# Set-up of a Mamba and expert block: weights loaded, folded and used in another order

## The chip, the cores and the metric

One core of a Trainium2 chip runs the whole program in one launch. The metric is the device time of one execution in microseconds. The core has five engines with an instruction queue each: PE (TensorE), DVE (VectorE), ACT (ScalarE), POOL (GpSimd) and SP (SyncE, which here only issues DMA transfers). They wait for each other by semaphores.

## What is computed

64 samples, each of 16 image tokens and 32 text tokens of width D = 192, go through an embedding, a two-way Mamba mixer and a layer of eight experts (two for each token). Cut to what matters here:

```python
# image: patches of 768 values, layer norm with gamma, beta, then a projection
h_img = _layernorm(patch) * gamma @ W_proj.T + (beta @ W_proj.T + b_proj)
# text: a token's row, a segment's row and two time embeddings (sine of an angle, last column linear)
angle = tau * w_tau + b_tau
h_txt = tok_rows + alpha_age * sin(angle_age) + alpha_abs * sin(angle_abs) + alpha_seg * seg_rows
x1 = _layernorm(h)
# mixer: x1 @ bm_in -> halves for the two directions -> Mamba (in_w, conv, silu, B, C, dt, scan, gate, out_w) -> bm_out
u = silu(conv(x)); dt = softplus(...); state = exp(dt * A) * state + dt * u * B; y = sum(state * C)
h2 = ln_g * _layernorm(mixer + x1) + ln_b + h
out = h2 + experts(_layernorm(h2))
```

Two weights are products that the kernel makes once at the start. `wxz` is the outer input projection times the Mamba's own (`bm_in` by `inT`, eight groups: two directions, two halves of the output, two halves of the contraction). `w2t` is the Mamba's output projection times the outer one (`outw` by `bmoT`). The layer norm of the image is folded too: `gw` is gamma times the projection, `proj_sum` its column sums, `proj_bias` is beta times the projection plus the bias.

## The kernel before

The tokens are cut into eight chunks of 384 (8 samples by 48). A chunk goes through the front (embedding, x1, its transpose `xT`), then for each direction through `xz` (PE: xT by wxz), the convolution (PE, with diagonal matrices `tap_diag`), silu, `bc`, `dt`, and 12 units of scan. A unit is 4 of 16 states by 128 of 384 channels: POOL makes the input `ring` = dtu times B (L645), ACT the decay in the two PSUM tiles `states` (L629, L632), DVE scans (L656) and multiplies by C (L658), PE sums over the states (L668). B and C come as broadcasts from DRAM (`brep`, `crep`, spread by SP, L608).

The order of all engines is written out by hand. Each engine first runs its own set-up function, then `program`: a list of steps `early()`, a wait for the whole set-up (`set_up`), `prologue()` (front and first direction of chunk 0), and a plan for each chunk. An engine takes from the list those steps for which it has a function.

The set-up before: SP issues all loads from one list (L839), `bm_in` and `inT` first, with a semaphore of their own (`fold_in`); behind them ids, taus and the patches of chunk 0 (`ptok`, `pT`, L275 to L278); then all others, which share one semaphore, `w_in`. PE folds eight groups into eight PSUM banks (L883), ACT copies each to `wxz` (L907). DVE waits for all of `w_in` (L862), makes the diagonals, `gw` and `betas`, and then takes up the patches. PE then makes proj_sum, proj_bias, the image (L311) and, still ahead of the embedding, the output weights' product (L897), which ACT copies to `w2t` behind the sine. POOL first gathers the text rows (L286), then waits for `w_in` and makes the angles `theta` (L336).

Of the kernel before, what the change touches and what calls it, by code (L numbers as in the profile page):

```python
# [22 lines left out]
KH = D // 2  # L23
# [48 lines left out]
def build_mamba(nc, a, dram, ident, logits, sem):  # L72

    with ExitStack() as ctx:
# [101 lines left out]
        fold_in = sem("folded_weights_loaded")  # L176
        w_in = sem("weights_loaded")
# [634 lines left out]
        def dve_router(v, c):  # L812
# [5 lines left out]
        loads = [  # L818
            (bm_in.rearrange("p d j k -> p (d j k)"), a["bm_in"]), (inT.rearrange("p j o -> p (j o)"), a["inT"]), (outw.rearrange("p j o -> p (j o)"), a["outw"]),
            (bmoT.rearrange("p j o -> p (j o)"), a["bmoT"]), (projT.rearrange("p k o -> p (k o)"), a["projT"]),  # L820
            (tgam, a["tgam"]), (tbet, a["tbet"]), (projb, a["projb"]),
            (xpw[:, :, 0:2 * NS], a["xpw_bc"]), (xpw[:, :, 2 * NS:2 * NS + R], a["xpw_dt"]), (dtw[2 * NS:2 * NS + R, :], a["dtw"]), (dtb[:], a["dtb"]),
            (cw[:].rearrange("p o k -> p (o k)"), a["cw"]), (cb[:], a["cb"]), (dskip[:], a["dskip"]),
            (aneg[:].rearrange("p o n -> p (o n)"), a["a_log"]),
            (w_tau[:].rearrange("p s k -> p (s k)"), a["w_tau"].partition_broadcast(128)),
            (b_tau[:].rearrange("p s k -> p (s k)"), a["b_tau"].partition_broadcast(128)),
            (alpha[:], a["alpha"].partition_broadcast(128)),
            (outb[:], a["outb"]), (ln_g[:], a["ln_g"].partition_broadcast(128)), (ln_b[:], a["ln_b"].partition_broadcast(128)),
            (rw[:].rearrange("p k e -> p (k e)"), a["rw"]),
        ]  # L830
        FOLDED = 2
        LOADED = 16 * (len(loads) - FOLDED)
        banks = [py] + [s[:, 512 * i:512 * i + 512] for s in states for i in range(2)] + [pf[0], pf[1], pq]

        def sp_setup(sp):
            for i, (dst, src) in enumerate(loads):
                if len(dst.shape) == 2 and len(src.shape) == 3:
                    src = src.rearrange("p a k -> p (a k)")
                sp.dma_start(dst, src).then_inc(w_in if i >= FOLDED else fold_in, 16)  # L839
                if i == FOLDED - 1:  # L840
                    sp_load(sp, 0)
# [8 lines left out]
        def dve_setup(v):  # L850
# [10 lines left out]
            v.wait_ge(set_dve, 2)  # L861
            v.wait_ge(w_in, LOADED)  # L862
            v.tensor_scalar(am[:], alpha[:, 0:2], mask[:], None, ALU.mult)
# [5 lines left out]
            for k in range(PD // 128):  # L869
                v.tensor_scalar(gw[:, k, :], projT[:, k, :], tgam[:, k:k + 1], None, ALU.mult)  # L870
                o = v.tensor_scalar(betas[:, k, :], ones[:], tbet[:, k:k + 1], None, ALU.mult)
            o.then_inc(set_dve, 1)
            v.wait_ge(set_act, 9)
            v.tensor_scalar(aneg[:], aneg[:], -1.0, None, ALU.mult).then_inc(set_dve, 1)

        def pe_setup(pe):
            pe.wait_ge(fold_in, 16 * FOLDED)
            i = 0
            for d in range(2):
                for k in range(2):  # L880
                    for h in range(2):
                        for j in range(2):
                            mm = pe.matmul(banks[i][0:KH + k, 0:DI], bm_in[:, d, j, KH * k:KH * (k + 1) + k], inT[:, j, DI * h:DI * h + DI], start=(j == 0), stop=(j == 1))  # L883
                        mm.then_inc(set_pe, 1)
                        i += 1
            pe.wait_ge(w_in, LOADED)
            pe.wait_ge(set_dve, 3)
            pe.wait_ge(set_act, 8)
# [5 lines left out]
            pe_img(pe, 0)  # L894
            for i in range(NC):
# [4 lines left out]
        def act_setup(act):  # L900
            act.preload_act_table_set("natural_log_exp_and_others")
            i = 0
            for d in range(2):
                for k in range(2):
                    for h in range(2):
                        act.wait_ge(set_pe, i + 1)
                        act.activation(wxz[0:KH + k, d, k, DI * h:DI * h + DI], banks[i][0:KH + k, 0:DI], ACT.Copy).then_inc(set_act, 1)  # L907
                        i += 1
            act.wait_ge(w_in, LOADED)
            act.activation(aneg[:], aneg[:], ACT.Exp).then_inc(set_act, 1)  # L910
            act.wait_ge(set_pe, 9)
            act.activation(proj_sum[:], pf[1][:, 0:D], ACT.Copy)
            act.activation(proj_bias[:], pf[0][:, 0:D], ACT.Copy).then_inc(set_act, 1)

# [806 lines left out]
```

## Time and profile before

| | |
|---|---|
| time, median of 3 runs | 1842.75 us (1842.67 to 1843.38) |
| profiled execution, its own time | 1843.9 us |
| span in its trace | 1842.1 us |
| PE busy | 1503.7 us, 82% of the span |
| DVE busy | 1361.4 us, 74% |
| POOL busy | 1087.9 us, 59% |
| ACT busy | 888.8 us, 48% |
| granted TensorE clock, mean | 0.911 of full |

The times in rows count from the start of the span. "Busy" is the time in which an engine has an instruction of its own in work; waits, branches and the issuing of transfers are not in it. A row of a timeline is a run of like instructions: start, microseconds, engine, line of the kernel, operation, what it writes and reads, how many, and in square brackets the idle time of the engine just before it and what released it. A float32 matmul leaves two records on PE.

### The profile page before, as it was taken

Reading aid. Unit: us, or ns where it says so; the run is one execution under the profiler, and the core shown is the slowest. Engines: PE = TensorE matmul, PEld = TensorE weight load, DVE = VectorE, ACT = ScalarE, POOL = GpSimd, SP = SyncE. Lnnn points to the kernel's source line nnn. Section 1 sums busy time; section 2 is a strip of 40 time slices with the busy share of each in tenths; the row PEclk is TensorE's granted clock in tenths of the full one; section 3 lists DMA queues with packets and bytes.
Section 4 is the critical chain, followed back from the end, with each engine's and each line's share of the span. In section 5 each row is a group of like instructions: output and inputs, shape, how many; then the busy total and the mean of one; then the engine's idle time right before and its main releaser. Section 6 shows DMA issues by size and latency. Waiting matters only on the chain. (4 is left out here: it accounts for less than half of the span.)

```text
span 1842.1 us, 20793 instructions
## 1 busy us (share of the span) xinstructions
PE 1503.7 (82%) x5318; PEld 891.8 (48%) x5319; DVE 1361.4 (74%) x1532; ACT 888.8 (48%) x1962; POOL 1087.9 (59%) x636
## 2 busy tenths in 40 slices
PE   5867887889788788968887897897663899999997
PEld 3434444445344444534544453453342566666665
DVE  4389999999999998998999999999956122222222
ACT  2455645656474655656565565755521222222221
POOL 2375776776777678777767877667710233333332
PEclk8789898899899889988998998998885999999999
DMA  3403122231321223041213303123003634344332
GB/s 88 162 21 137 69 78 104 77 137 36 135 77 71 85 92 139 21 149 52 95 62 110 145 19 135 53 86 127 26 15 114 217 88 88 83 93 84 84 91 52
DMA packets 60432, 165.77 MB, mean 90 GB/s; under 512 B 17086, under 2 KB 29100, under 8 KB 60364
## 3 DMA queue, kind: packets, MB, share of 16 engines
q1 hardware_dynamic: 48220, 148.91, 23.5%
q0 software_dynamic: 12144, 16.13, 4.9%
q8 instruction: 21, 0.34, 0.1%
q14 instruction: 47, 0.39, 0.1%
HBM read 152.98 MB, written 12.03 MB: 90 GB/s over the span
## 5 line engine op out<-in xcount | busy, mean ns | idle before, releaser
L645 POOL TENSOR_TENSOR ring<-dtu,brep 128x1536 f32<-128x1536 f32 x192 | 669.0, 3487 | 273.5 <-DVE states L656 231.0
L668 PE MATMUL py<-ring,ident 128*128 128x384 f32 x1536 | 612.0, 547 | 204.3 <-ACT yg L681 130.3
L656 DVE TENSOR_TENSOR_SCAN states<-states,ring 128x768 f32<-128x768 f32 x384 | 673.7, 1755 | 46.9 <-ACT states L632 29.7
L668 PEld LDWEIGHTS py<-ring,ident 128*128 128x128 f32 x1536 | 309.7, 211 | 482.2 <-issue 143.4
L632 ACT ACTIVATE states<-dt_,aneg 128x376 f32<-128x376 f32 x768 | 406.2, 560 | 0.0
L658 DVE TENSOR_TENSOR ring<-states,crep 128x768 f32<-128x768 f32 x384 | 367.6, 957 | 13.2
L629 ACT ACTIVATE states<-zero_cols 128x16 f32<-128x16 f32 x384 | 70.7, 184 | 464.4 <-DVE ring L658 459.9
L1378 DVE COPY yidx<-place 128x1 int32 (+1 forms) x56 | 8.4, 154 | 245.7 <-DMA out_tokens<-ys,yidx 245.7
L1305 POOL DMA_INDIRECT xs<-x_scratch,yidx x56 | 55.4, 990 | 227.7 <-DVE yweight L1384 153.3
L1332 PE MATMUL gu<-w,xsT 128*128 x440 | 155.3, 496 | 5.0 <-issue 4.4
L467 PE MATMUL pf<-xT,wxz 97*128 97x384 f32 (+1 forms) x384 | 145.2, 517 | 7.6 <-ACT zs L482 4.9
L1343 ACT ACTIVATE act_g<-gu 128x768 f32<-128x768 f32 x55 | 44.6, 811 | 198.2 <-PE gu L1337 198.2
L1394 POOL DMA_INDIRECT out_tokens<-ys,yidx x55 | 87.3, 1588 | 78.9 <-issue 42.9
L492 PE MATMUL pf<-xc,tap_diag 128*128 128x384 f32 x384 | 130.9, 489 | 0.0
L1366 PE MATMUL yps<-wd,hidT 128*128 x660 | 117.0, 327 | 1.0 <-ACT hidT L1360 1.0
L1332 PEld LDWEIGHTS gu<-w,xsT 128*128 128x128 f32 x440 | 80.3, 193 | 65.4 <-issue 62.3
L640 POOL TENSOR_TENSOR dtu<-dt_,u 128x384 f32<-128x384 f32 x48 | 48.4, 1009 | 104.2 <-DVE dt_ L593 104.2
L467 PEld LDWEIGHTS pf<-xT,wxz 97*128 97x128 f32 (+1 forms) x384 | 76.9, 204 | 68.1 <-issue 11.1
L1366 PEld LDWEIGHTS yps<-wd,hidT 128*128 128x128 f32 x660 | 106.5, 191 | 1.6 <-issue 1.6
L492 PEld LDWEIGHTS pf<-xc,tap_diag 128*128 128x128 f32 x384 | 72.6, 189 | 53.3 <-issue 1.1
L1360 ACT ACTIVATE hidT<-hps 128x768 f32<-128x768 f32 x55 | 44.6, 811 | 104.2 <-PE hps L1354 104.2
L1337 PE MATMUL gu<-rest,xsT 64*128 64x256 f32 (+1 forms) x440 | 87.5, 517 | 5.7 <-DMA rest<-in_w_rest 5.7
(228 smaller groups left out, 1566.5 us busy)
## 6 DMA issues: line engine op xcount, KB each, us to landing
brep<-b_c_rows SPq DMA_DIRECT2D x64, 768.0 KB, 4.0
crep<-b_c_rows SPq DMA_DIRECT2D x64, 768.0 KB, 5.9
rest<-in_w_rest SPq DMA_DIRECT2D x55, 384.0 KB, 3.2
w<-in_w SPq DMA_DIRECT2D x8, 768.0 KB, 8.4
wd<-in_wd SPq DMA_DIRECT2D x8, 576.0 KB, 9.3
ptok<-in_p_tok SPq DMA_DIRECT2D x8, 384.0 KB, 4.0
pT<-in_p_T SPq DMA_DIRECT2D x8, 384.0 KB, 4.7
out_tokens<-h SPq DMA_DIRECT2D x8, 288.0 KB, 2.1
```

What stands on the lines that cost most here:

```text
L467: mm = pe.matmul(p[:, 0:T], wxz[0:rows, d, k, 128 * o:128 * o + 128], xT[0:rows, k].rearrange("p b l -> p (b l)"), start=(k == 0), stop=(k ...
L492: mm = pe.matmul(p[:, 0:T], tap_diag[:, o, k, :], xc[:, o, :, at:at + L], start=(k == 0), stop=(k == KC))
L629: act.activation(start, zero_cols[:].unsqueeze(2), ACT.Copy)
L632: op = act.activation(x0[:, k, :, lo:lo + L - 1], src, ACT.Exp, scale=aneg[:, o, n:n + 1])
L645: gp.tensor_tensor(ring[:, w % NRING], dtu[:, d, o, :].unsqueeze(1).to_broadcast([128, GN, T]), brep[:, ng], ALU.mult).then_inc(dbu_ok, 1)
L656: v.tensor_tensor_scan(h_in, h_in, x_in, 0.0, ALU.mult, ALU.add).then_inc(scan_ok, 1)
L658: v.tensor_tensor(x, h, half_of(crep[:, ng], i), ALU.mult).then_inc(hc_ok, 1)
L668: mm = pe.matmul(py[:, 0:T], ident[:], ring[:, w % NRING, i, :], start=(ng == 0 and i == 0), stop=False)
L1332: pe.matmul(gate_up[i][:, lo:hi], xsT[:, b, 0, :], w13[:, bass.ds(e, 1), HF * i + lo:HF * i + hi].rearrange("p a n -> p (a n)"), start=Tru ...
L1337: mm = pe.matmul(gate_up[i][:, lo:hi], xsT[rows, b, 1, :], rest[rows, b, lo:hi], start=False, stop=True)
L1366: mm = pe.matmul(yps[:, 0:D], hidT[:, b, 128 * k:128 * k + 128], wd[:, bass.ds(e, 1), k, :].rearrange("p a n -> p (a n)"), start=(k == 0), ...
L1394: gp.indirect_dma_start(dram["out"], bass.IndirectOffsetOnAxis(ap=yidx[:, r:r + 1], axis=0), ys[:, b, :], None, compute_op=ALU.add).then_i ...
```

## The change

It puts the set-up into another order, on all five engines.

- Loads: SP issues ids and taus first, then the angle weights (`w_tau`, `b_tau`, `alpha`) with a semaphore of their own (`tau_in`), then `bm_in` and `inT`, `ptok`, and all others. ACT issues the projection (`tgam`, `projT`, `tbet`, `projb`, semaphore `proj_in`) and `pT` on its own queue, ahead of everything else that it does.
- DVE makes `gw` and `betas` when `proj_in` is there, then takes up the patches and the angles; the diagonals and the sign of `aneg` come behind that, just ahead of the embedding.
- PE folds two of the eight groups (`SOON`), makes proj_sum, proj_bias and the image, then folds the other six. The groups use five PSUM banks in turn, so the sixth and later ones wait for ACT to have read an earlier one. ACT reads the six behind the sine.
- POOL makes the angles first and gathers the text rows behind them.
- `set_up` is waited for only behind xT, so the embedding of chunk 0 doesn't wait for the folded weights. The output weights' product moves into the prologue, between dt2 and z01 on PE; ACT copies it just ahead of the first decay.
- The input of the first unit (dtu and ring) is made by DVE (`dve_input`); POOL starts with the second.

PE in the set-up, first before and then in the changed kernel (`py`, `states`, `pf`, `pq` are PSUM tiles; `ring` holds the fold loads, `brep` and `crep` the projection):

```order
L883 MATMUL py<-ring 96x384 x2
L883 MATMUL states<-ring 96x384 x2
L883 MATMUL states<-ring 97x384 x4
L883 MATMUL states<-ring 96x384 x2
L883 MATMUL pf<-ring 96x384 x2
L883 MATMUL pf<-ring 97x384 x2
L883 MATMUL pq<-ring 97x384 x2
L890 MATMUL pf<-gw,ones 128x192 x6
L892 MATMUL pf<-brep,crep 128x192 x6
L893 MATMUL pf<-crep,ones 128x192
L311 MATMUL pq<-gw,pT 128x192 x6
L897 MATMUL py<-ring 128x192 x2
```

```order
L914 MATMUL py<-ring 96x384 x2
L914 MATMUL states<-ring 97x384 x2
L934 MATMUL pf<-gw,ones 128x192 x6
L936 MATMUL pf<-brep,crep 128x192 x6
L937 MATMUL pf<-crep,ones 128x192
L313 MATMUL pq<-gw,pT 128x192 x6
L914 MATMUL states<-ring 96x384 x2
L914 MATMUL states<-ring 97x384 x2
L914 MATMUL states<-ring 96x384 x2
L914 MATMUL py<-ring 97x384 x2
L914 MATMUL states<-ring 96x384 x2
L914 MATMUL states<-ring 97x384 x2
```

Six groups have moved from ahead of proj_sum to behind the image, and the output weights' product (L897) no longer follows the image.

ACT from proj_sum to the first normalization (`hrs`), before and now:

```order
L912 ACTIVATE proj_sum<-pf 128x192
L913 ACTIVATE proj_bias<-pf 128x192
L376 ACTIVATE prs<-pmv,eps 128x1
L378 ACTIVATE prs<-prs 128x1
L379 ACT_TABLE_LOAD
L382 ACTIVATE resid<-resid,halfpi 128x2x191
L382 ACTIVATE resid<-resid 128x2x191
L384 ACT_TABLE_LOAD
L385 ACTIVATE resid<-theta 128x4
L919 ACTIVATE w2t<-py 128x192
L919 ACTIVATE w2t<-states 128x192 x2
L424 ACTIVATE hrs<-hmv,eps 128x3
```

```order
L386 ACT_TABLE_LOAD
L387 ACTIVATE resid<-theta 128x4
L952 ACTIVATE aneg<-aneg 128x48
L925 ACTIVATE wxz<-states 96x384
L925 ACTIVATE wxz<-states 97x384
L925 ACTIVATE wxz<-states 96x384
L925 ACTIVATE wxz<-py 97x384
L925 ACTIVATE wxz<-states 96x384
L925 ACTIVATE wxz<-states 97x384
L426 ACTIVATE hrs<-hmv,eps 128x3
```

The second list starts at the sine's last table load. Behind the angles' copy (L387) now stand the Exp of `aneg` and the reads of six groups, where before the three reads of w2t stood; `hrs` waits behind all of them on ACT.

POOL from the angles of chunk 0 to those of chunk 1, before and now (`ring` of three units and of two):

```order
L336 TENSOR_SCALAR theta<-w_tau,taus 128x192 x4
L340 TENSOR_TENSOR theta<-theta,b_tau 128x384 x2
L640 TENSOR_TENSOR dtu<-dt_,u 128x384
L645 TENSOR_TENSOR ring<-dtu,brep 128x1536 x3
L286 DMA tok_rows<-in_tok_emb,ids 128x192
```

```order
L338 TENSOR_SCALAR theta<-w_tau,taus 128x192 x4
L342 TENSOR_TENSOR theta<-theta,b_tau 128x384 x2
L288 DMA tok_rows<-in_tok_emb,ids 128x192
L289 DMA seg_rows<-in_seg_emb,ids 128x192
L288 DMA tok_rows<-in_tok_emb,ids 128x192
L289 DMA seg_rows<-in_seg_emb,ids 128x192
L649 TENSOR_TENSOR ring<-dtu,brep 128x1536 x2
L288 DMA tok_rows<-in_tok_emb,ids 128x192
```

Chunk 0's gathers now stand behind theta, and dtu with the first unit's ring has left POOL; it stands on DVE between the last dt_ step and the first scan.

The core of the diff:

```diff
+            if isinstance(c, int) and c == 0 and w == 1:
+                gp.wait_ge(dbu_ok, 1)
...
+        def dve_input(v):
+
+            v.wait_ge(dv.sem, dv.after("dt", 0))
+            v.tensor_tensor(dtu[:, 0, 0, :], dt_[:, 0, 0, :], u[:, 0, 0, :], ALU.mult).then_inc(dtu_ok, 1)
+            v.wait_ge(dtu_ok, 1)
+            v.wait_ge(brep_in[0], 16)
+            v.tensor_tensor(ring[:, 0], dtu[:, 0, 0, :].unsqueeze(1).to_broadcast([128, GN, T]), brep[:, 0], ALU.mult).then_inc(dbu_ok, 1)
...
+        banks = [py] + [s[:, 512 * i:512 * i + 512] for s in states for i in range(2)]
+        GROUPS = [(d, k, h) for d in range(2) for h in range(2) for k in range(2)]
+        SOON = 2
...
+            sp.dma_start(ids[:], a["ids"][0:1].rearrange("a p k -> p (a k)")).then_inc(ids_in, 16)
+            sp.dma_start(taus[:], a["taus"][0:1].rearrange("a p k -> p (a k)")).then_inc(ids_in, 16)
+            for dst, src in tau_loads:
+                sp.dma_start(dst, src).then_inc(tau_in, 16)
+            for dst, src in fold_loads:
+                sp.dma_start(dst, src).then_inc(fold_in, 16)
+            sp.dma_start(ptok[:], a["p_tok"][0:1].rearrange("a p k -> p (a k)")).then_inc(patch_in, 16)
+            for dst, src in loads:
+                sp.dma_start(dst, src).then_inc(w_in, 16)
+
+        def act_loads(act):
+            for dst, src in proj_loads:
+                act.dma_start(dst, src).then_inc(proj_in, 16)
+            act.dma_start(pT[:].rearrange("p k t -> p (k t)"), a["p_T"][0:1].rearrange("a p k -> p (a k)")).then_inc(patch_in, 16)
...
             v.wait_ge(set_dve, 2)
+            v.wait_ge(proj_in, 16 * len(proj_loads))
+            for k in range(PD // 128):
+                v.tensor_scalar(gw[:, k, :], projT[:, k, :], tgam[:, k:k + 1], None, ALU.mult)
...
+            v.wait_ge(tau_in, 16 * len(tau_loads))
+            v.tensor_scalar(am[:], alpha[:, 0:2], mask[:], None, ALU.mult)
+
+        def dve_diagonals(v):
             v.wait_ge(w_in, LOADED)
...
-            v.wait_ge(set_act, 9)
+            v.wait_ge(set_act, SOON + 2)
             v.tensor_scalar(aneg[:], aneg[:], -1.0, None, ALU.mult).then_inc(set_dve, 1)
...
+                if i >= len(banks):
+                    pe.wait_ge(set_act, SOON_DONE(i - len(banks)))
...
         def early():
             yield "phase", 0, 0
+            yield "rows", 0, 0
             yield "reduce", 0, 0
+            yield "diagonals", 0, 0
             yield "sin", 0, 0
-
-        def prologue():
+            yield "rest", 0, 0
             for step in ("embed", "embed_rs", "x1", "xT", "xT_out"):
                 yield step, 0, 0
 
+        def prologue():
...
+            yield "fold_out", 0, 0
...
+            yield "input", 0, 0
+            for w in range(1, AHEAD):
                 yield "ahead", 0, w
```

## Rows read from the trace of the kernel before

**Rows 1.** Busy time by stretch: engines (records), granted TensorE clock, DMA share, GB/s.

```profile
2.00:10.00 8.00, 3.46 (x6) 1.68 (x7) 1.32 (x10) 0.57 (x2) 1.83 (x2) 1.00 1.02 293
10.00:18.00 8.00, 8.00 (x23) 3.94 (x22) 0.40 (x3) 2.44 (x5) 2.38 (x4) 1.00 0.85 210
44.00:53.00 9.00, 8.37 (x17) 4.83 (x18) 0.00 (x0) 2.09 (x6) 0.00 (x0) 0.50 0.01 2
100.00:1270.00 1170.00, 953.11 (x2872) 529.71 (x2871) 1100.34 (x1017) 700.38 (x1613) 851.53 (x454) 0.92 0.25 88
```

**Rows 2.** Timeline of PE in the set-up.

```profile
6.54 2.88 PE L883 MATMUL py<-ring 96*96 96x384 f32 x4 [6.54 <-DMA ring<-in_inT]
...
25.64 3.94 PE L890 MATMUL pf<-gw,ones 128*128 128x192 f32 x12 [5.78 <-DVE aneg L874]
29.42 2.11 PE L892 MATMUL pf<-brep,crep 128*128 128x192 f32 x12
...
34.04 0.82 PE L897 MATMUL py<-ring 96*128 96x192 f32 x4
...
43.94 1.49 PE L443 MATMUL pf<-ident,x_new 128*96 128x128 f32 x6 [7.79 <-DVE x_new L435]
46.06 7.62 PE L467 MATMUL pf<-xT,wxz 96*128 96x384 f32 x12 [0.63 <-ACT xT L454]
```

**Rows 3.** Timeline of ACT in the set-up.

```profile
12.02 0.49 ACT L907 ACTIVATE wxz<-states 96x384 f32<-96x384 f32 x1 [2.07 <-PE states L883]
...
19.90 0.49 ACT L907 ACTIVATE wxz<-pq 97x384 f32<-97x384 f32 x1 [0.80 <-PE pq L883]
...
32.09 0.33 ACT L912 ACTIVATE proj_sum<-pf 128x192 f32<-128x192 f32 x1 [11.57 <-PE pf L893]
...
36.70 0.21 ACT L385 ACTIVATE resid<-theta 128x4 f32<-128x4 f32 x1
...
42.27 0.30 ACT L424 ACTIVATE hrs<-hmv,eps 128x3 f32<-128x3 f32 x1 [4.69 <-DVE hmv L419]
```

**Rows 4.** Timeline of DVE in the set-up.

```profile
17.60 0.23 DVE L863 TENSOR_SCALAR am<-alpha,mask 128x2 f32<-128x2 f32 x1 [13.87 <-DMA rw<-in_rw]
...
22.16 1.06 DVE L870 TENSOR_SCALAR gw<-brep,crep 128x192 f32<-128x192 f32 x1
...
25.56 1.01 DVE L318 BATCH_NORM_STATS2 pst<-ptok 128x6 f32<-128x384 f32 x2
...
37.68 0.41 DVE L391 SCALAR_TENSOR_TENSOR img_t<-proj_sum,pneg,pq 128x192 f32<-128x192 f32 x1 [5.61 <-ACT w2t L919]
```

**Rows 5.** Timeline of all engines around the first scans.

```profile
72.29 0.45 SPq L276 DMA_DIRECT2D taus<-in_taus  x1
...
74.52 1.36 DVE L593 TENSOR_TENSOR dt_<-dt_,ea 128x1152 f32<-128x1152 f32 x1
75.91 0.19 ACT L629 ACTIVATE states<-zero_cols 128x16 f32<-128x16 f32 x1 [3.00 <-DVE dt_ L593]
...
77.12 10.22 POOL L645 TENSOR_TENSOR ring<-dtu,brep 128x1536 f32<-128x1536 f32 x3
...
105.07 1.74 DVE L359 SCALAR_TENSOR_TENSOR resid<-turns,theta 128x768 f32<-128x768 f32 x1 [5.71 <-POOL turns L353]
```

**Rows 6.** Issues of transfers, 0 to 12 us: queue, count, KB, us to landing.

```profile
ring<-in_inT SPq DMA_DIRECT2D x1, 576.0 KB, 5.2
brep<-in_projT SPq DMA_DIRECT2D x1, 576.0 KB
...
pT<-in_p_T SPq DMA_DIRECT2D x1, 384.0 KB, 5.5
ring<-in_bm_in SPq DMA_DIRECT2D x1, 289.5 KB, 3.3
...
w_tau<-in_w_tau SPq DMA_DIRECT2D x1, 192.0 KB
```

**Rows 7.** Issues of transfers at 72.3 us, the same columns.

```profile
taus<-in_taus SPq DMA_DIRECT2D x1, 2.0 KB, 14.0
```

More of the change, by code:

```diff
@@ L817, in build_mamba @@
         block = ctx.enter_context(nc.Block())
[L818 to L824, printed above, removed]
+        fold_loads = [(bm_in.rearrange("p d j k -> p (d j k)"), a["bm_in"]), (inT.rearrange("p j o -> p (j o)"), a["inT"])]
+        tau_loads = [
             (w_tau[:].rearrange("p s k -> p (s k)"), a["w_tau"].partition_broadcast(128)),
@@ L868, in dve_setup, with pe_fold_in, SOON_DONE, act_fold_in @@
                     v.tensor_scalar(tap_diag[:, o, k, :], ident[:], cw[:, o, k:k + 1], None, ALU.mult)
[L869 to L872, printed above, removed]
[L873 to L886 removed]
+            v.wait_ge(set_act, SOON + 2)
+            v.tensor_scalar(aneg[:], aneg[:], -1.0, None, ALU.mult).then_inc(set_dve, 1)
+            v.wait_ge(set_dve, 4)
+        def pe_fold_in(pe, some):
+            for i in some:
+                d, k, h = GROUPS[i]
+                if i >= len(banks):
+                    pe.wait_ge(set_act, SOON_DONE(i - len(banks)))
+                for j in range(2):
+                    mm = pe.matmul(banks[i % len(banks)][0:KH + k, 0:DI], bm_in[:, d, j, KH * k:KH * (k + 1) + k], inT[:, j, DI * h:DI * h + DI], start=(j == 0), stop=(j == 1))
+                mm.then_inc(set_pe, 1)
+        def SOON_DONE(i):
+            return i + 1 if i < SOON else i + 3
+        def act_fold_in(act, some):
+            for i in some:
+                d, k, h = GROUPS[i]
+                act.wait_ge(set_pe, i + 1 if i < SOON else i + 2)
+                act.activation(wxz[0:KH + k, d, k, DI * h:DI * h + DI], banks[i % len(banks)][0:KH + k, 0:DI], ACT.Copy).then_inc(set_act, 1)
+        def pe_setup(pe):
+            pe.wait_ge(fold_in, 16 * len(fold_loads))
+            pe_fold_in(pe, range(SOON))
+            pe.wait_ge(proj_in, 16 * len(proj_loads))
             pe.wait_ge(set_dve, 3)
[L888 removed]
+            pe.wait_ge(set_pool, 3)
             for k in range(PD // 128):
@@ L894, in pe_setup, with act_setup, act_rest, pe_fold_out @@
             pe_img(pe, 0)
+            pe_fold_in(pe, range(SOON, len(GROUPS)))
+            pe.wait_ge(set_act, SOON + 1)
+        def act_setup(act):
+            act_loads(act)
+            act.preload_act_table_set("natural_log_exp_and_others")
+            act_fold_in(act, range(SOON))
+            act.wait_ge(set_pe, SOON + 1)
+            act.activation(proj_sum[:], pf[1][:, 0:D], ACT.Copy)
+            act.activation(proj_bias[:], pf[0][:, 0:D], ACT.Copy).then_inc(set_act, 1)
+        def act_rest(act):
+            act.wait_ge(w_in, LOADED)
+            act.activation(aneg[:], aneg[:], ACT.Exp).then_inc(set_act, 1)
+            act_fold_in(act, range(SOON, len(GROUPS)))
+        def pe_fold_out(pe):
             for i in range(NC):
@@ L898, in pe_setup @@
             mm.then_inc(set_pe, 1)
[L900 to L913, printed above, removed]
         def act_w2t(act):
-            act.wait_ge(set_pe, 10)
+            act.wait_ge(set_pe, len(GROUPS) + 2)
             for i in range(NC):
@@ L1056, in program @@
             run(eng, steps, early())
-            if "folded" in steps:
-                steps["folded"](eng)
             set_up(eng)
```

41 lines of the change are left out of this document (25 added, 16 removed).

## The prediction

> **What bounds the kernel now.** First a table by stretch [rows 1]: in the eight chunks (100 to 1270 us) DVE is busy 1100 of 1170 us, and behind them lies a stage of its own. Both go through in a fixed order, and the first is next to full on one engine, so a start that comes earlier should reach the end whole. The change touches what lies ahead of the first scans, where no engine is full. So the second view is the timeline of each engine through the set-up. PE [rows 2] folds eight groups from 6.54 on, stands still for 5.78 us, makes proj_sum, proj_bias and the image from 25.64 to 34.04, folds the output weights, and stands still again until the transposes of x1 at 43.94. ACT [rows 3] reads proj_sum at 32.09; the angles' sine follows up to 36.91. DVE [rows 4] shows what came first: it waited 13.87 us for the last of all weight loads, built the diagonals (17.60 to 22.16), then gw and betas, and only at 25.56 took up the patches. One semaphore for all loads, and diagonals ahead of gw: that is the critical chain of the set-up. The third view, the chunk's first steps on all engines [rows 5], starts at T = 75.88, the end of the last dt_ step on DVE (74.52 + 1.36), and shows that DVE waits there for POOL until 105.07.
>
> I call the start of the x1 transposes X (43.94 before). What the change gives is the shift of X, the shift of T against X, and what happens behind T.
>
> **X, step by step.** The fold loads. Before, bm_in and inT came first, 865.5 KB [rows 6]. From 2 us on the DMA engines were at a share of 1.02 and 293 GB/s [rows 1], which moves 0.886 MB by 5.0; PE started at 6.54, so 1.5 us lie between the last byte and PE. Now ids, taus, w_tau, b_tau (192 KB each) and alpha stand ahead of them on SP, 1255 KB up to inT's last byte, and ACT issues projT (576 KB), pT (384) and three small ones at the same time, 967 KB. Where the engines are full already, a second queue adds no bytes per us, it only shares. With even shares ACT's 967 KB are through before SP's 1255: 2.275 MB at 293 GB/s are 7.8 us, and inT is there at 2 + 7.8 + 1.5 = 11.3. If SP's stream isn't held up at all, its 1.285 MB give 7.9. At the 210 GB/s of 10 to 18 us, where small and broadcast loads ran [rows 1], it would be 14.3. I take 11.3: full engines speak for sharing, and most of these bytes are large loads, as in the faster stretch.
>
> The Trainium skill says it outright (DMA: Bandwidth & Descriptors, "Issuing engines are not separate DMA queues"): DMAs started from different engines run on the same 16 DMA engines and interleave, and starting them from several saves only the issue time. By that rule the second queue brings no bandwidth, and inT lands at the shared time; if each queue had a bandwidth of its own, it would be the 7.9. The share of 1.02 agrees with the rule, but no run here has two such queues yet.
>
> From 11.3 on PE works without a gap. Two groups with the clock not yet fast took 5.3 us before (6.54 to 11.8; ACT reads the second at 12.02): 16.6. gw and betas, 3.4 us on DVE (22.16 to 25.56), need only the projection and are made by then. proj_sum ran at 1.2 GHz before (25.64 to 29.42, 3.78), proj_bias with as many matmuls at 2.4 took 2.11. PE is warm now, so proj_sum, proj_bias and the image take 2.11 + (34.04 - 29.42) = 6.7: 23.3. Six groups at the spacing of ACT's reads (12.02 to 19.90, six steps of 1.31): 7.9, so 31.2. The eighth waits for a bank that ACT has freed by then. ACT reads the last at 31.4 and is free at 31.8; hrs, x1 and the hand-off to PE took 1.67 (42.27 to 43.94), so X = 33.5.
>
> Beside it runs a chain of ACT and DVE. ACT read proj_sum 1.95 ahead of the image's end, so now at 21.35; from there to the end of the angles' copy were 4.82 (32.09 to 36.91): 26.2. Exp of aneg, now behind the sine, 26.4; DVE's sign of it 26.6; then the embedding, img_t to hrs 4.59 (37.68 to 42.27): 31.2. That is 0.6 under ACT's 31.8 above: the two chains nearly tie. DVE's other work is covered: patches (2.67 MB up to ptok's end, 12.6), 6.5 us from their statistics to the clamp (25.56 to 32.07, where the idle of 5.61 begins), 4.6 of diagonals: 23.7, against the 26.4 for which it must wait anyway. If that cover were gone, each us beyond it would cost one. So the six groups "behind the image" are not hidden: with them PE is the end of the path, and the gain is that diagonals, waits and a stretch at 1.2 GHz have left it. X moves by 43.94 - 33.5 = 10.4.
>
> **X to T.** Nothing in this chain changes but the clock. Before, PE was at 1.2 GHz behind both idle stretches: proj_sum above behind 5.78 us, and xz behind 7.79, with a granted clock of 0.50 from 44 to 53 us [rows 1]. Now the gap ahead of the transposes is 33.5 - 31.2 = 2.3 us. At its start the clock is at 2.4; whether it falls in it no row tells. If it holds, xz takes 0.56 (2.11 by 3.78) of its 7.62 us, 3.4 less. I take "falls, but later than before", because more idle than work lies between 31.2 and xz, and put 0.5 us for transposes that still run fast; bounds 0 and 3.4. Folding the output weights on PE behind dt2 is 12 records, four of which took 0.82 at 2.4: some 2.2 us, or 4.4 at 1.2. It delays z01, which ACT reads only behind the first decay, after T. ACT's w2t falls into the 3.00 us in which ACT waited for dt_ [rows 5]. Price 0; without that cover w2t's three reads, each of proj_sum's size (0.33), would delay the first decay by 1.0.
>
> **Behind T.** The first dtu and ring step go from POOL to DVE. POOL's three rings ended at 77.12 + 10.22 = 87.34, T+11.5, the first of them at T+4.7. DVE took 1.36 for 1152 elements, so some 0.5 for dtu's 384 and 1.8 for the ring's 1536: 2.4 with hand-offs. POOL's two rings then end at T+9.3. But its next step gathers chunk 1's rows, and their ids land only at 72.29 + 14.0 = 86.3 [rows 5, 7], T+10.4, behind the spreads. So of 2.2 us at most 1.1 remain, and at least 0 if the gather starts as late after its ids as before; I take 0.7. POOL leads until turns is done, and the end of DVE's wait of 5.71 us at 105.07 moves by that much. DVE's second scan waits for ACT and lies ahead of that wait, so what it gains or loses is swallowed there.
>
> **Sum.** 10.4 + 0.5 + 0.7 = 11.6. Against the profiled execution's 1843.9 that is 1832.3; that one lies 1.15 above the median of the runs, 1842.75, so for the median 1831.2.
>
> **Rivals.** (a) The clock holds through the gap. For it: the gap is shorter than either of the two behind which PE was slow. Against it: more idle than work. 2.9 better than forecast: 1828.3. Chance 0.22. (b) SP's stream isn't held up by ACT's: inT at 7.9, all behind it 3.4 earlier (the image needs patches at 12.6, and PE gets to it at 17.9): 1827.8. Against it the share of 1.02. Chance 0.12. (c) The loads run at 210 GB/s: 3.0 later, 1834.2. Chance 0.10. (d) The change does at the start what it says, but a later wait takes the shift back: 1839 to 1843. Against it DVE's 94% in the chunks. Chance 0.05. (e) Slower than before: the projection comes late on ACT's queue, which issued no transfer before, so that no row prices it. DVE needs it 3.4 us ahead of PE's 16.6, at 13.2; each us behind that costs one, the gain is gone at 24.8, and 0.2% is lost from 28.5 on. All loads of before were there at 17.60 [rows 4]. Chance 0.02. The forecast itself, 1829.5 to 1833.5, has 0.47; 0.02 are unnamed.
>
> **How the numbers follow.** The range 1826 to 1835 takes in (a), (b), (c) and the bounds of the clock and of POOL's step; (d), (e) and sums of two deviations are left out, some 0.12. About 0.2% (3.7 us) is what a measurement of this kernel can tell from no change. Faster 0.95: all but (e) and most of (d); same 0.03; slower 0.02.
>
> **What would show it.** PE's first group near 11.3 and no gap on PE from there to 31; gw ahead of the patches on DVE; ACT's last read of a group just ahead of hrs; X near 33.5; the granted clock at X, 1.2 or 2.4, decides (a). T near 65, POOL's first gather of chunk 1 right behind its ids, DVE's reduce near T+28.5. I am wrong if PE waits for DVE in the set-up, if hrs comes over 1 us behind ACT's last group, or if the span behind the reduce differs from that of before by more than 1 us.

## The result, and the profile after

The changed kernel takes 1831.94 us (median of 3 runs, 1830.27 to 1832.87) against 1842.75: ratio 0.9939, 95% interval 0.9916 to 0.9962, some 11 us faster. The forecast was 1831.2, with a range of 1826 to 1835. The profiled execution took 1832.87 us, its span is 1831.1 (1842.1 before), its mean granted clock 0.919 (0.911).

The total is right. Its parts are less so, and the profile says which. First the table by stretch, with the columns of [rows 1]:

```profile
2.00:10.00 8.00, 0.00 (x0) 0.00 (x0) 3.79 (x22) 1.28 (x1) 0.39 (x1) 1.00 0.73 219
10.00:18.00 8.00, 3.69 (x6) 1.82 (x7) 2.54 (x8) 0.49 (x1) 7.14 (x9) 1.00 1.10 222
...
38.00:42.00 4.00, 3.76 (x6) 2.19 (x7) 0.00 (x0) 0.50 (x1) 0.00 (x0) 0.50 0.00 0
...
100.00:1270.00 1170.00, 956.20 (x2881) 531.73 (x2882) 1109.17 (x1023) 697.61 (x1612) 850.93 (x453) 0.92 0.25 90
```

From 2 to 10 us the DMA engines are no longer full: a share of 0.73 and 219 GB/s, where before it was 1.02 and 293. The third row lies in xz, at a granted clock of 0.50, the lower of the two levels (1.2 of 2.4 GHz). The chunks are as full on DVE as they were.

The timeline of PE in the set-up answers [rows 2]:

```profile
14.31 2.87 PE L914 MATMUL py<-ring 96*96 96x384 f32 x4 [14.31 <-DMA ring<-in_inT]
16.98 2.77 PE L914 MATMUL states<-ring 96*97 96x384 f32 x4
19.54 2.48 PE L934 MATMUL pf<-gw,ones 128*128 128x192 f32 x12
...
31.63 2.74 PE L914 MATMUL states<-ring 96*96 96x384 f32 x8
36.46 0.83 PE L445 MATMUL pf<-ident,x_new 128*96 128x128 f32 x6 [2.09 <-DVE x_new L437]
38.24 7.05 PE L469 MATMUL pf<-xT,wxz 96*128 96x384 f32 x12 [0.94 <-ACT xT L456]
```

From 14.31 to 34.37 (31.63 + 2.74) no row shows a wait, and the transposes follow 2.09 us behind. So X is 36.46, and from the first group to X are 22.15 us; the forecast had 22.2 (11.3 to 33.5). But the first group comes 3.0 us later than forecast: inT is late. xz takes 7.05, at half clock almost throughout.

ACT, for [rows 3], shows the end of that path:

```profile
29.14 0.21 ACT L387 ACTIVATE resid<-theta 128x4 f32<-128x4 f32 x1
...
34.41 0.49 ACT L925 ACTIVATE wxz<-states 97x384 f32<-97x384 f32 x1 [0.80 <-PE states L914]
34.80 0.29 ACT L426 ACTIVATE hrs<-hmv,eps 128x3 f32<-128x3 f32 x1
```

hrs starts right behind the last read of a group. DVE, for [rows 4] and for its part of [rows 5]:

```profile
7.53 1.46 DVE L889 TENSOR_SCALAR gw<-brep,crep 128x192 f32<-128x192 f32 x6 [3.80 <-DMA crep<-in_projb]
...
15.91 1.02 DVE L320 BATCH_NORM_STATS2 pst<-ptok 128x6 f32<-128x384 f32 x2 [5.28 <-DMA ptok<-in_p_tok]
...
29.74 0.41 DVE L393 SCALAR_TENSOR_TENSOR img_t<-proj_sum,pneg,pq 128x192 f32<-128x192 f32 x1
...
66.23 1.36 DVE L595 TENSOR_TENSOR dt_<-dt_,ea 128x1152 f32<-128x1152 f32 x1
67.62 0.56 DVE L654 TENSOR_TENSOR dtu<-dt_,u 128x384 f32<-128x384 f32 x1
68.22 1.76 DVE L657 TENSOR_TENSOR ring<-dtu,brep 128x1536 f32<-128x1536 f32 x1
...
96.21 1.74 DVE L361 SCALAR_TENSOR_TENSOR resid<-turns,theta 128x768 f32<-128x768 f32 x1 [5.44 <-POOL turns L355]
```

T is 66.23 + 1.36 = 67.59. DVE's new work takes 0.56 + 1.76, as costed. The reduce, which ended DVE's wait for POOL, starts at 96.21, which is T+28.62; before it was T+29.19 (105.07 - 75.88).

POOL behind T:

```profile
70.24 6.82 POOL L649 TENSOR_TENSOR ring<-dtu,brep 128x1536 f32<-128x1536 f32 x2 [49.64 <-DVE ring L657]
78.71 0.98 POOL L288 DMA_INDIRECT tok_rows<-in_tok_emb,ids  x1 [1.65 <-DMA taus<-in_taus]
```

Its two rings end at 77.06, and the gather of chunk 1's rows then waits 1.65 us for the ids and taus, as the prediction had it.

Issues of transfers, in the columns of [rows 6]:

```profile
ring<-in_inT SPq DMA_DIRECT2D x1, 576.0 KB, 10.6
...
taus<-in_taus SPq DMA_DIRECT2D x1, 2.0 KB, 3.3
```

The table of the queues from 2 to 4, 4 to 6 and 10 to 12 us, two rows each: packets, MB, share of the 16 engines' time. q1 is SP's queue, q10 ACT's:

```profile
q10 hardware_dynamic: 192, 0.37, 66.0%
q1 hardware_dynamic: 228, 0.00, 5.8%
...
q1 hardware_dynamic: 165, 0.22, 30.7%
q10 hardware_dynamic: 149, 0.23, 30.1%
...
q1 hardware_dynamic: 110, 0.49, 104.5%
q10 hardware_dynamic: 3, 0.00, 0.1%
```

inT was issued at 3.63 and landed at 14.2. From 2 to 4 us SP's queue moved next to nothing (228 packets, under 0.005 MB, 5.8% of the engines' time), while ACT's had 66%. In packets the two are nearly even (228 and 192); SP's were rows of 16 bytes, ACT's some 1900 bytes each (0.37 MB by 192).

The account of the profiled execution, in shifts against before: X 43.94 - 36.46 = 7.48 (forecast 10.4); X to T 31.94 - 31.13 = 0.81 (0.5); T to the reduce 29.19 - 28.62 = 0.57 (0.7). The reduce is thus 8.86 earlier, where 11.6 were forecast. The span is 11.0 shorter: 2.1 us were gained behind the reduce, for which the prediction had no term. So in this execution two deviations of 2 to 3 us cancel, and that the total meets the forecast within 1 us is in part luck.

### The profile page after: what moved, and what is told of

It is laid out like the page before. It is cut to its first block and busy times, and to the rows that moved or that the text cites. A ratio compares the mean times of both kernels' runs of the same rounds, so it can differ in the third digit from the quotient of the medians.

```text
span 1831.1 us, 20797 instructions
## 1 busy us (share of the span) xinstructions
PE 1496.4 (82%) x5318; PEld 887.5 (48%) x5319; DVE 1362.5 (74%) x1534; ACT 888.1 (48%) x1962; POOL 1083.0 (59%) x634
## 5 line engine op out<-in xcount | busy, mean ns | idle before, releaser
L469 PE MATMUL pf<-xT,wxz 97*128 97x384 f32 (+1 forms) x384 | 141.4, 506 | 9.5 <-ACT zs L484 6.4
```

Source lines behind the costliest of these rows:

```text
L469: mm = pe.matmul(p[:, 0:T], wxz[0:rows, d, k, 128 * o:128 * o + 128], xT[0:rows, k].rearrange("p b l -> p (b l)"), start=(k == 0), stop=(k ...
```

## The experiments

**The changed kernel again, and one part of it undone at a time.** Three variants ran beside a repeat of the changed kernel; before was 1842.81 us there.

The repeat, with no edit:

> The changed kernel once more, for its own spread. X (start of the x1 transposes) was 36.46 and inT landed at 14.3; the shift against before was 8.9 us at the first scan behind chunk 1's reduce, and 11.0 us at the end. If the further 2.1 us are a matter of the run (where PE's clock happens to fall in the chunks), this profile shows the same X, the same 8.9 within 0.2, and another end shift, between 8 and 12. If they belong to the change, the end shift is 11 again.

Measured: 1834.73 us (1831.33 to 1835.2), ratio 0.995 (0.9938 to 0.9962). First group 13.77, X 35.39, T 66.37, reduce 95.09, span 1832.9. The reduce is 9.98 earlier than before, the span only 9.2 shorter. So the 2.1 us gained behind the reduce in the first execution are not a part of the change: here 0.8 are lost there. The set-up was expected to repeat within 0.2 us and did not: X is 1.07 us earlier, 0.54 of it by inT's landing and the rest in PE's first products. A difference of about 1 us at X between two single executions is thus no finding by itself.

The first unit's input given back to POOL:

```diff
-            yield "input", 0, 0
-            for w in range(1, AHEAD):
+            for w in range(AHEAD):
```

> The change, but the first unit's dtu and ring stay on POOL. My theory: what DVE's two operations give is capped by the landing of chunk 1's ids, so DVE's reduce of chunk 1 starts 0.6 us later against T (T+29.2 instead of T+28.6), and the time is 0.6 us longer than the changed kernel's. Rival: the whole 2.2 us of POOL's work count, and it is 2.2 us longer. Second rival: nothing, within 0.3 us.

Measured: 1833.06 us, ratio 0.9951 (0.9939 to 0.9963), T 65.03, reduce 94.12. POOL:

```profile
66.27 10.22 POOL L647 TENSOR_TENSOR ring<-dtu,brep 128x1536 f32<-128x1536 f32 x3
76.63 0.98 POOL L288 DMA_INDIRECT tok_rows<-in_tok_emb,ids  x1
```

and DVE:

```profile
94.12 1.74 DVE L361 SCALAR_TENSOR_TENSOR resid<-turns,theta 128x768 f32<-128x768 f32 x1 [6.41 <-POOL turns L355]
```

The three rings are back, 10.22 us, and the gather follows without a wait for its ids. The reduce is at T+29.09, as before (29.19); in the changed kernel and its repeat it is at T+28.62 and T+28.72. So the move of the input to DVE is worth 0.4 to 0.5 us there, close to the theory's 0.6; the table below has 29.09 to 29.19 for the input on POOL, 28.56 to 28.94 and once 29.75 for it on DVE. It lets POOL's rings end 2.0 us earlier against T (77.06 - 67.59 = 9.5, against 76.49 - 65.03 = 11.5), and 1.65 of these become the wait for ids. In the time of the kernel that can't be told from the rivals' 0 and 2.2: 1833.06 lies between the two medians of the changed kernel, 1831.94 and 1834.73.

All eight groups ahead of the projection, or none:

```diff
-        SOON = 2
+        SOON = 8
```

> The change, but all eight folded groups ahead of proj_sum and the image (SOON 8). My theory: proj_sum comes 7.8 us later, and the chain of sine, aneg, embedding and hrs hangs on it: X = 43.9 instead of 36.5, so 7.4 us longer than the changed kernel. Rival, if the order of groups and image doesn't matter because PE's whole work ends the path either way: X moves by less than 1 us.

> The change, but no folded group ahead of proj_sum and the image (SOON 0): PE no longer waits for inT before proj_sum. My theory, inT's late landing at 14.3 sets the path: proj_sum starts at 10.3, the image ends near 19, eight groups end near 29.5, X near 31.7 instead of 36.5, 4.8 us shorter than the changed kernel. Rival, the patches' landing at 15.9 and DVE's chain behind it set X: then X is no earlier than 34, at most 2.5 us shorter.

Measured with 8: 1841.23 us, ratio 0.9994 (0.9985 to 1.0002). ACT:

```profile
30.27 0.33 ACT L947 ACTIVATE proj_sum<-pf 128x192 f32<-128x192 f32 x1 [3.93 <-PE pf L937]
```

and PE:

```profile
13.32 2.88 PE L914 MATMUL py<-ring 96*96 96x384 f32 x4 [13.32 <-DMA ring<-in_inT]
...
30.16 2.22 PE L313 MATMUL pq<-gw,pT 128*128 128x192 f32 x12
41.65 1.49 PE L445 MATMUL pf<-ident,x_new 128*96 128x128 f32 x6 [9.27 <-DVE x_new L437]
```

With 0 (the diff reads `SOON = 0`): 1833.73 us, ratio 0.9948 (0.9935 to 0.9961), X 35.38. PE's first product:

```profile
13.69 4.21 PE L934 MATMUL pf<-gw,ones 128*128 128x192 f32 x12 [13.69 <-DMA ring<-in_inT]
```

This run doesn't test what was expected of it. The wait for inT stands at the head of PE's set-up and is still there, so proj_sum starts at 13.69 as before and not at 10.3. What it would give to start the projection without inT stays open; what the run compares is the place of the first two groups alone.

With eight groups ahead, proj_sum is read at 30.27, the sine and the embedding stand behind it with nothing on PE beside them, and PE is idle for 9.27 us: X is 28.3 us behind the first group (41.65 - 13.32). With two ahead it is 22.15, with none 21.7. So the six groups behind the image carry 6 us of the shift, because they run beside the sine and the embedding; whether the first two stand ahead of the projection or behind, with inT awaited first in both, does not matter. The theory for eight groups had X at 43.9: its direction is right, its size 2.3 too much, 1.0 of this by inT's earlier landing. All other parts together are worth 2.3 us at X (43.94 - 41.65): from the first group to X 9.1 us are gone (37.40 before, 28.33 here), and inT's later landing takes 6.8 of them back. The gap of 9.27 us is again followed by a slow xz (6.09 us), and the time of that kernel can't be told from that of before.

**The diagonals alone, in the kernel before.** gw and betas are made ahead of the diagonals, with nothing else changed:

```diff
-            for o in range(NC):
-                v.tensor_scalar(skip_diag[:, o, :], ident[:], dskip[:, o:o + 1], None, ALU.mult)
-                for k in range(KC + 1):
-                    v.tensor_scalar(tap_diag[:, o, k, :], ident[:], cw[:, o, k:k + 1], None, ALU.mult)
             for k in range(PD // 128):
...
             o.then_inc(set_dve, 1)
+            for o in range(NC):
+                v.tensor_scalar(skip_diag[:, o, :], ident[:], dskip[:, o:o + 1], None, ALU.mult)
...
```

> The kernel before with one part of the change alone: on DVE gw and betas ahead of the diagonals, all loads and waits as before. PE then starts proj_sum 4.5 us earlier, but the sine still waits for DVE's clamp, which does not move (32.07): the sine's end moves from 36.9 to 34.5, X by 2.4 us, so 2.4 us shorter than before. If PE alone set the path, it would be 4.5; if the patches' order is what counts, 0.

Measured: 1841.19 us against 1843.61, ratio 0.9992 (0.9983 to 1.0001). X 42.02, T 73.22, reduce 102.39: 1.92, 2.66 and 2.68 us earlier. gw starts at 17.79 instead of 22.16, but X gains less than half of these 4.4 us, as the patches' chain on DVE then stands behind the diagonals. The 2.4 us expected at X are thus nearly met; in the time of the kernel they can't be told from no change. The order on DVE alone is a small part of the change.

**Which load makes inT late.** Four orders of the loads. First, the folded weights at the head of SP's queue:

```diff
+            for dst, src in fold_loads:
+                sp.dma_start(dst, src).then_inc(fold_in, 16)
             sp.dma_start(ids[:], a["ids"][0:1].rearrange("a p k -> p (a k)")).then_inc(ids_in, 16)
...
-            for dst, src in fold_loads:
-                sp.dma_start(dst, src).then_inc(fold_in, 16)
```

> The change, but SP issues bm_in and inT ahead of ids, taus and the angle weights. Theory A, bytes shared at 293 GB/s: inT lands by 8.6, PE starts then, patches land at 15.9 as now and become the bound through DVE's clamp and ACT's sine: X near 31.5, 5 us shorter than the changed kernel. Theory B, it is the small and broadcast transfers at the head of SP's queue that held the large ones up, not the bytes: inT lands near 7, and the patches too come later or earlier by 1 us at most. If X doesn't move, the late inT was not on the path.

Measured: 1829.99 us against 1843.61, ratio 0.9926 (0.9913 to 0.994). PE:

```profile
8.53 2.88 PE L914 MATMUL py<-ring 96*96 96x384 f32 x4 [8.53 <-DMA ring<-in_inT]
...
31.04 1.49 PE L445 MATMUL pf<-ident,x_new 128*96 128x128 f32 x6 [3.29 <-DVE x_new L437]
33.36 7.44 PE L469 MATMUL pf<-xT,wxz 96*128 96x384 f32 x12 [0.83 <-ACT xT L456]
```

The first group is 5.8 us earlier than in the changed kernel, X 5.4 (5.2 and 4.4 against the repeat). So inT's landing sets X nearly one to one, although theta now is later (DVE waits 2.88 us for it, up to 16.49). Theory A's 8.6 and 31.5 are met and theory B's 7 is not: with the large loads first, the prediction's sharing holds (289 GB/s from 2 to 10 us in this run). But the loads that went behind them are 0.4 MB, 1.4 us at that rate, and the first group moved by 5.2 to 5.8. Bytes alone don't explain the order of the changed kernel.

Second, all loads on SP, in this order: ids, taus, the projection, the angle weights, the folded weights, ptok, pT, the others:

```diff
+            for dst, src in proj_loads:
+                sp.dma_start(dst, src).then_inc(proj_in, 16)
             for dst, src in tau_loads:
...
+            sp.dma_start(pT[:].rearrange("p k t -> p (k t)"), a["p_T"][0:1].rearrange("a p k -> p (a k)")).then_inc(patch_in, 16)
...
-            act_loads(act)
```

> The change, but all loads on SP, in the order ids, taus, projection, angle weights, bm_in, inT, ptok, pT, rest. Theory A, two queues only share: inT no longer has pT ahead of it and lands near 10, X near 32, 4 us shorter than the changed kernel. Rival, the second queue was worth its issue time and its overlap: inT at 14 or later, X no earlier than 36.5.

Measured: 1834.47 us against 1843.61, ratio 0.9949 (0.9936 to 0.9963). First group 13.40, X 35.62, span 1834.4:

```profile
13.40 2.87 PE L917 MATMUL py<-ring 96*96 96x384 f32 x4 [13.40 <-DMA ring<-in_inT]
...
taus<-in_taus SPq DMA_DIRECT2D x1, 2.0 KB, 1.7
```

inT is there as early on one queue as on two (13.77 and 14.31), although projT and three more loads now stand ahead of it and pT behind. Both numbers of the expectation are missed (10, and 14 or later). The order changed together with the number of queues, so the run doesn't price the second queue alone; in the time it brings nothing that can be shown. The Trainium skill (DMA: Bandwidth & Descriptors, "Issuing engines are not separate DMA queues") says that transfers started by several engines run on the same 16 DMA engines and that only issuing time is saved. Nothing in these runs speaks against that. One thing did change: taus landed in 1.7 us, where it took 3.2 to 4.9 in the eight executions that have it at the head with ACT's queue beside it.

Third and fourth, alpha alone moved behind ptok, and then w_tau and b_tau moved behind inT as well, with ids and taus still first:

```diff
-            (alpha[:], a["alpha"].partition_broadcast(128)),
         ]
...
         loads = [
+            (alpha[:], a["alpha"].partition_broadcast(128)),
...
-            for dst, src in tau_loads:
-                sp.dma_start(dst, src).then_inc(tau_in, 16)
             for dst, src in fold_loads:
                 sp.dma_start(dst, src).then_inc(fold_in, 16)
+            for dst, src in tau_loads:
+                sp.dma_start(dst, src).then_inc(tau_in, 16)
```

> Only alpha's load (12 bytes for each of 128 partitions) goes from its place ahead of bm_in to the place behind ptok; the product with it goes behind the last load. Theory A (the drag on inT, 14.2 in place of the forecast 11.3, is that of the smallest rows, alpha's): bm_in and inT land 1.5 us earlier or more, inT at 12.5 or before, first folded group there, transposes at 34.5 or before. Theory B (it is that of the two broadcasts of 192 KB, each 128 copies of one row, which leave the engines half idle): inT lands within 0.5 us of 13.3 to 14.2, transposes at 35.0 to 36.5. Time in both within 1.5 us of the changed kernel.

> As the run before, and the two broadcast loads w_tau and b_tau go behind bm_in and inT; ids and taus (16 bytes for each partition) stay first. Theory B (the broadcasts are the drag, ids and taus cost their two issues and little more): first folded group at 8.5 to 9.8, share of the DMA engines 0.9 or more from 3 to 9 us, transposes at 31.0 to 32.2, ratio 0.992 to 0.994. Theory A' (any load of many tiny rows at the head of a queue holds what is behind it): first folded group at 10.5 or later, transposes at 33 or later. Theta leaves POOL within 1 us of its time in the run with the folded weights first, so DVE's chain is what ends last.

Measured with alpha late: 1833.15 us against 1842.86, ratio 0.9949 (0.9934 to 0.9965), first group 13.39, X 34.47. Theory A falls by its own number for inT (12.5): inT lands where it landed in the other runs of the changed kernel's order (13.05 to 14.31). X is at theory A's bound (34.5) and not in theory B's range, but the run with the input on POOL, with alpha ahead, had 34.16, so X doesn't decide here. Yet the engines are busier from 5 to 8 us. The table by stretch for this run:

```profile
5.00:6.00 1.00, 0.00 (x0) 0.00 (x0) 0.00 (x0) 0.00 (x0) 0.00 (x0) 1.00 0.89 120
6.00:7.00 1.00, 0.00 (x0) 0.00 (x0) 0.35 (x2) 0.00 (x0) 0.00 (x0) 1.00 0.89 267
7.00:8.00 1.00, 0.00 (x0) 0.00 (x0) 1.00 (x5) 0.00 (x0) 0.00 (x0) 1.00 1.07 368
```

and for the changed kernel:

```profile
5.00:6.00 1.00, 0.00 (x0) 0.00 (x0) 0.00 (x0) 0.00 (x0) 0.00 (x0) 1.00 0.38 126
...
7.00:8.00 1.00, 0.00 (x0) 0.00 (x0) 0.47 (x3) 0.00 (x0) 0.00 (x0) 1.00 0.56 190
```

So the idle engines of that stretch go with alpha's rows of 12 bytes (with alpha ahead the six executions of that order had shares of 0.38 to 0.75 from 5 to 6 us), and from 6 us on the bytes move faster too. But inT gains 0.4 to 0.9 us by it at most (against 13.77 and 14.31), no more than the runs differ.

Measured with the broadcasts behind: 1830.98 us, ratio 0.9935 (0.9921 to 0.9949). PE:

```profile
10.40 2.88 PE L913 MATMUL py<-ring 96*96 96x384 f32 x4 [10.40 <-DMA ring<-in_inT]
...
33.03 0.83 PE L445 MATMUL pf<-ident,x_new 128*96 128x128 f32 x6 [2.09 <-DVE x_new L437]
```

and the two queues from 2 to 4 us:

```profile
q10 hardware_dynamic: 144, 0.35, 77.2%
q1 hardware_dynamic: 169, 0.00, 4.5%
```

10.40 lies between the bounds of the two theories (up to 9.8, from 10.5) and closer to the second's, and X at 33.03 is the second's. So both loads cost: the broadcasts ahead of inT 3.0 us (13.39 to 10.40), ids and taus 1.9 more (10.40 to 8.53; 1.5 against the 8.89 of the last experiment), half of it their two issues (bm_in is issued at 1.75 instead of 0.81). At the 293 GB/s of [rows 1] these 1.9 us would move 0.56 MB, and ids and taus have 4 KB. These are single executions, and one order of loads spread over 1.3 us (13.05 to 14.31). The rest fits what the queues' rows show, that SP's queue moves next to nothing until 4 us while rows of 16 bytes are on it. The two queues again went through nearly as many packets (169 and 144), and with no second queue taus landed in 1.7 us. That fits two queues that take turns by packets, so that a queue of tiny rows gets few bytes beside one of large rows; no run here varied this alone, so it is not shown. In this run 1.0 us of the shift is lost behind T: the reduce is at T+29.75, and the first scan waited 3.02 us for its loads (1.47 in the changed kernel). I have not followed that further.

**The clock.** Six idle matmuls of gw and ones stand on PE between the last folded group and the transposes; the wait for ACT's eighth count keeps them from writing `py` before its last group is read:

```diff
-            pe.wait_ge(set_act, SOON + 1)
+            pe.wait_ge(set_act, 8)
+            for k in range(6):
+                pe.matmul(py[:, 0:D], ones[:], gw[:, k, :], start=True, stop=True)
```

> The change with six idle matmuls (128x192, results unused) on PE between the last folded group and the transposes, so that PE works through most of the gap of 2.1 us. If the clock fell because of that gap, it now stays at 2.4 GHz, xz takes 3.9 instead of 7.05 us, and the time is 3.2 us shorter than the changed kernel; the idle matmuls end at 36.4 and delay the transposes by 0.2 at most. Rival: the gap between transposes and xz alone is enough for the clock to fall, or it has to do with the kind of work, and the time is the same within 0.5 us.

Measured: 1832.24 us against 1843.61, ratio 0.9931 (0.9917 to 0.9944). PE:

```profile
33.54 2.12 PE L942 MATMUL py<-gw,ones 128*128 128x192 f32 x12
35.70 0.86 PE L445 MATMUL pf<-ident,x_new 128*96 128x128 f32 x6
37.50 4.12 PE L469 MATMUL pf<-xT,wxz 96*128 96x384 f32 x12 [0.94 <-ACT xT L456]
```

and the table by stretch:

```profile
38.00:42.00 4.00, 4.00 (x14) 2.36 (x13) 0.00 (x0) 1.34 (x3) 0.00 (x0) 1.00 0.00 0
```

With the gap filled the granted clock stays 1.00, xz takes 4.12 us in place of 7.05, and X to T 28.41 in place of 31.13. So the clock alone was worth 2.7 us from X to T (2.6 against the repeat), and the changed kernel did not have them: its 2.09 us of idle ahead of the transposes were followed by the lower level. The rival falls, as the gap between the transposes and xz is still there (0.94). In the time of the kernel the gain can't be told from the changed kernel's spread: 0.9931 (0.9917 to 0.9944) against 0.9939 and 0.995, with intervals that overlap.

**Both together.** The folded weights first and eight idle matmuls:

```diff
+            for dst, src in fold_loads:
+                sp.dma_start(dst, src).then_inc(fold_in, 16)
...
+            pe.wait_ge(set_act, 8)
+            for k in range(8):
+                pe.matmul(py[:, 0:D], ones[:], gw[:, k % 6, :], start=True, stop=True)
```

> The folded weights' two loads stand first on SP's queue (as in the run before it that did this) and eight idle matmuls of 192 columns stand on TensorE between the last folded group and the first transpose. Theory (the set-up's end is the landing of inT plus a fixed chain, and the half clock at the first layer's product costs 2.7 us by itself, so that the two gains add): first folded group at 8.5, transposes at 31.0 to 31.3, granted clock 1.00 from 30 to 50, transposes to the end of the first unit's input 28.4 in place of 32.1, that end at 59.5, the first scan behind the reduce at 95.7 (99.3 with the loads' order alone, 100.2 with the idle matmuls alone), time 1826.5, ratio 0.991. Rival (the early start runs into the loads of B and C or into POOL's turns): the reduce waits over 7 us for POOL or the first scan over 4 us for its loads, and the first scan behind the reduce stays at 97.5 or later, ratio 0.9925 or more.

Measured: 1827.6 us (1824.05 to 1829.14) against 1842.86, ratio 0.9915 (0.9902 to 0.9929). PE:

```profile
31.20 0.86 PE L445 MATMUL pf<-ident,x_new 128*96 128x128 f32 x6 [0.66 <-DVE x_new L437]
33.00 4.12 PE L469 MATMUL pf<-xT,wxz 96*128 96x384 f32 x12 [0.94 <-ACT xT L456]
```

and the table by stretch:

```profile
31.00:46.00 15.00, 12.99 (x43) 7.48 (x44) 0.14 (x1) 6.43 (x13) 0.00 (x0) 1.00 0.00 1
```

T is 59.42 (59.5 expected), the reduce 88.04 (T+28.62), the first scan behind it 95.44 (95.7 expected), the time 1.1 us above the expected one. In the set-up the two gains add, and the rival doesn't hold. This version has the lowest median of the study; its interval lies below that of the changed kernel's repeat (0.9938 to 0.9962) but overlaps those of the folded weights first, of the idle matmuls and of the broadcasts behind, so the time alone doesn't rank it before these.

All executions beside each other. X, T and reduce are starts in the profile, the shift is that of the reduce against the one profiled execution of before, the gain is the time before times one minus the ratio:

| kernel | first group | X | X to T | T to reduce | shift | gain |
|---|---|---|---|---|---|---|
| before | 6.54 | 43.94 | 31.94 | 29.19 | | |
| changed | 14.31 | 36.46 | 31.13 | 28.62 | 8.9 | 11.2 |
| changed, repeat | 13.77 | 35.39 | 30.98 | 28.72 | 10.0 | 9.2 |
| input on POOL | 13.05 | 34.16 | 30.87 | 29.09 | 10.9 | 9.0 |
| eight groups ahead | 13.32 | 41.65 | 30.72 | 28.56 | 4.1 | 1.1 |
| none ahead | 13.69 | 35.38 | 30.99 | 28.72 | 10.0 | 9.6 |
| folded weights first | 8.53 | 31.04 | 32.07 | 28.81 | 13.1 | 13.6 |
| one queue | 13.40 | 35.62 | 31.18 | 28.94 | 9.3 | 9.4 |
| idle matmuls | 13.33 | 35.70 | 28.41 | 28.65 | 12.3 | 12.7 |
| before, gw first | 6.45 | 42.02 | 31.20 | 29.17 | 2.7 | 1.5 |
| both | 8.89 | 31.20 | 28.22 | 28.62 | 17.0 | 15.7 |
| alpha late | 13.39 | 34.47 | 30.87 | 28.67 | 11.1 | 9.4 |
| broadcasts behind | 10.40 | 33.03 | 31.38 | 29.75 | 10.9 | 12.0 |

## Why the prediction was right, point by point

**A start that comes earlier reaches the end.** Right. Summed over the twelve rows of the table (eleven kernels, one of them twice) the shifts are 120 us and the gains 114. Single ones differ by up to 3 us either way, about the spread of a kernel's own runs, and the span behind the reduce is 1734.9 to 1739.4 us in the twelve executions against 1737.0 before. So (d) falls. The bound that I set in advance, that this span differs by no more than 1 us from that of before, was too narrow: it differs by 2.1 in the first execution and by 0.8 the other way in the repeat, so by the prediction's own sign the first execution would have shown it wrong. Why the span behind the reduce varies was not followed.

**inT's landing.** This is the term that was mis-sized. "Where the engines are full already, a second queue adds no bytes per us, it only shares": the engines were not full. The bytes were about right (8 us at 219 GB/s and 2.8 at 222 are 2.37 MB by 12.8 us, 1.5 ahead of PE's start; 2.275 were taken); the rate taken for them, 293 GB/s, was that of two large loads with nothing small ahead. With the rows of 16 bytes and the two broadcasts at the head of SP's queue it was 219, and the first group came at 14.31 (13.77 in the repeat), the time of rival (c), where 210 GB/s gave 14.3. So what rival (c) supposed, with a chance of 0.10, is what the loads did, and its 1834.2 is nearer to the repeat's 1834.73 than the forecast. The order of the experiments takes this apart: 8.5 without these loads ahead, 10.4 with ids and taus, 13.4 with the broadcasts. That ACT's bytes go through ahead of SP's was right (from 10 us on q10 has 0.1%), and rival (b) falls, as inT came at 14.3 and not at 7.9.

**From the first group to X.** Right: 22.15 us against 22.2, with the order of events as told (PE without a gap, the last read of a group, hrs, x1). The first two groups took 5.23 us where 5.3 were taken from before; the first needs 2.87 us, the later ones some 1.4, though the table's clock column reads 1.00 from 10 to 18 us too. The run with eight groups ahead completes the reason given. The gain was said to be that "diagonals, waits and a stretch at 1.2 GHz have left" the path. From the first group to X these are 9.1 us (37.40 to 28.33). Another 6.2 (28.33 to 22.15) come of the six groups, which now run beside the sine and the embedding; the prediction did not count that as a gain by itself. Of the 15.3 the later landing of inT took 7.8 back, which leaves the 7.48.

**X to T.** The case was right: the clock fell, later than before. Price 0.5, measured 0.81 and 0.96 in the repeat; the upper bound of 3.4 was 3.5 when the clock was kept (31.94 - 28.41). Rival (a) falls for this kernel, and its price is real. The output weights' product cost nothing that shows.

**Behind T.** 0.7 forecast, 0.57 and 0.47 measured, for the reason given: POOL's next step waits for its ids. The run with the input back on POOL takes it away (0.10). One run with DVE's input, the broadcasts behind, lost it too.

**The sum.** 8.9 and 10.0 us at the reduce, of 11.6 forecast, as inT's 3 us are missing and little came in elsewhere. That the first median lay 10.8 below before and not nearer 9 goes with the 2.1 us that its profiled execution gained behind the reduce, and is luck; the repeat's ratio gives 9.2. (e) falls: the projection was there at 7.53 on DVE.

## What to carry to other kernels

Cost a load by what stands ahead of it on its own queue: here a few KB of tiny rows (beside a second, busy queue) or two broadcasts at the head held it as long as hundreds of KB of large rows. So put the large load that something waits for first, and price a queue from a stretch with the same kinds of rows. When work is moved behind something, look for what it then runs beside: a chain on two other engines was the cover that paid here. And where the profile shows the lower clock behind a short gap of TensorE, fill the gap with idle matmuls that cannot delay the next real one: that was worth 2.7 us on the path of the set-up here, about a quarter of what the whole change gave. And test an order of loads by the landing that something waits for, since the time of the kernel can't tell 2 us from its own spread here.

## What the runs showed of the hardware that was not expected

- A load of 2 KB in rows of 16 bytes (taus) at the head of SP's queue landed in 3.2 to 4.9 us in the eight executions with a busy second queue, and in 1.7 with one queue. From 2 to 4 us of the changed kernel SP's queue had 5.8% of the engines' time and ACT's 66.0%, with 228 and 192 packets: there the queues were near even in packets and not in bytes. From 4 to 6 us, with the broadcasts on SP's queue, they were even in time too (30.7% and 30.1%).
- The share of the DMA engines alone says little of progress: with alpha moved it was 0.89 instead of 0.38 from 5 to 6 us, at nearly the same rate (120 and 126 GB/s). From 7 to 8 us the rate rose with it (368 against 190), and the load that was waited for still landed at 13.39, no earlier than the others.
- Gaps of 2.09 us (seven executions of six kernels) and 3.29 us (one) on TensorE ahead of the transposes were all followed by an xz of 6.24 to 7.44 us; with the gap cut to 0.66 us or to none by idle matmuls the granted clock stayed at 1.00 and xz took 4.12.
